# Last attention of a four-layer block: TensorE turns one unit in eight instead of one in four, VectorE and DMA turn all four units of every second half

## The reference

```python
xn = layer_norm(x, g1, b1)                    # x: the context, (4, 512, 256)
ln_lat = layer_norm(latents, g2, b2)          # latents: the tokens, (4, 512, 256)
q = ln_lat @ Wq                               # 16 heads of 64
kv = jnp.concatenate([xn, ln_lat], axis=1) @ Wkv      # 1024 keys
weight = jnp.einsum('bhld,bhnd->bhln', q * scale, k * scale)
weight = jnp.where(full_mask[:, None, None, :], weight, neg)
weight = jax.nn.softmax(weight.astype(jnp.float32), axis=-1)
out = jnp.einsum('bhln,bhnd->bhld', weight, v)
return out @ Wout
```

## Time and profile before

| | |
|---|---|
| runs | 2943.0, 2953.18, 2944.42 us; median 2944.42 |
| profiled execution | 2945.35 us, span 2943.6 |
| granted TensorE clock, mean | 0.92 of full |
| TensorE busy | 2481.0 us, 84% of the span |
| VectorE busy | 1828.4 us, 62% |
| ScalarE busy | 1170.7 us, 40% |
| GpSimd busy | 755.3 us, 26% |
| DMA | 257.06 MB, mean 87 GB/s |
| transfers of the last attention (L791) | 1024 of 96 KB: 784 by SyncE, 240 by ScalarE |

### The profile page before, as it was taken

How to read it: one execution, slowest core, us unless ns; L and a number is a source line. 1 busy time by engine, 2 the same in 40 slices (tenths; PEclk the granted TensorE clock), 3 DMA queues, 4 the chain that set the end, 5 groups by cost and what they waited for, 6 DMA issues and landing times. The chain is left out here.

```text
span 2943.6 us, 35609 instructions
## 1 busy us (share of the span) xinstructions
PE 2481.0 (84%) x12608; PEld 1335.9 (45%) x12608; DVE 1828.4 (62%) x4072; ACT 1170.7 (40%) x2095; POOL 755.3 (26%) x462
## 2 busy tenths in 40 slices
PE   6888972865888699889899979989988989997996
PEld 2333331323555344545554635554454545463554
DVE  5667745246867474477767357748437875835774
ACT  1433430212323153265544146635325653514662
POOL 1002352520000042043323023414203432402441
PEclk8999985875878799999999999999999999999998
DMA  7411006974200200244320124430023442012442
GB/s 226 136 37 21 11 15 206 316 249 150 87 8 3 106 1 1 87 108 119 97 79 8 73 61 118 116 111 11 8 88 100 116 108 79 1 52 71 110 125 73
DMA packets 112959, 257.06 MB, mean 87 GB/s; under 512 B 36198, under 2 KB 56294, under 8 KB 106762
## 3 DMA queue, kind: packets, MB, share of 16 engines
q1 hardware_dynamic: 93978, 220.26, 24.8%
q10 hardware_dynamic: 12656, 25.97, 3.6%
q0 software_dynamic: 6144, 8.48, 1.0%
HBM read 119.81 MB, written 29.69 MB: 51 GB/s over the span
## 5 line engine op out<-in xcount | busy, mean ns | idle before, releaser
L858 POOL TENSOR_SCALAR pbuf<-pbuf,recip 128x1024 f32<-128x1024 f32 x128 | 364.5, 2848 | 946.0 <-DVE recip L762 946.0
L807 ACT ACTIVATE pbuf<-ps,least 128x1024 f32<-128x1024 f32 x256 | 284.3, 1113 | 295.3 <-DVE least L755 219.5
L755 DVE CUSTOM_DVE_ANT_0 ps<-ps,mask 128x1024 f32<-128x1024 f32 x256 | 307.9, 1244 | 140.2 <-PE ps L687 139.2
L584 POOL TENSOR_SCALAR pbuf<-pbuf,recip 128x512 f32<-128x512 f32 x128 | 200.2, 1576 | 459.7 <-DVE recip L505 459.7
L687 PE MATMUL ps<-kH,qT 64*128 64x512 f32 x1024 | 267.4, 642 | 49.8 <-ACT pbuf L807 47.0
L712 PE MATMUL ps<-work,vh 128*64 128x256 f32 x2048 | 251.9, 390 | 0.0
L555 ACT ACTIVATE pbuf<-ps,least 128x512 f32<-128x512 f32 x256 | 172.7, 686 | 155.6 <-DVE least L495 155.6
L769 DVE STREAM_TRANSPOSE pbuf<-pbuf 128x2048 f32<-128x2048 f32 (+1 forms) x128 | 226.3, 1768 | 0.0
L1554 ACT ACTIVATE early<-ps 128x1536 f32<-128x1536 f32 x86 | 123.9, 1441 | 200.9 <-PE ps L1369 191.7
L1632 DVE TENSOR_REDUCE mh<-ps 128x3 f32<-128x1536 f32 x86 | 150.0, 1744 | 63.8 <-PE ps L1358 61.2
L712 PEld LDWEIGHTS ps<-work,vh 128*64 128x64 f32 x2048 | 138.3, 138 | 95.2 <-issue 36.6
(11 more groups left out here) (371 smaller groups left out, 4054.7 us busy)
## 6 DMA issues: line engine op xcount, KB each, us to landing
work<-pbuf SPq DMA_DIRECT2D x784, 96.0 KB, 2.5
work<-pbuf ACTq DMA_DIRECT2D x240, 96.0 KB, 2.9
early<-in_L_wgu SPq DMA_DIRECT2D x22, 768.0 KB
expert_rows<-zero_rows SPq DMA_DIRECT2D x16, 1024.0 KB, 11.5
yg<-expert_rows SPq DMA_DIRECT2D x16, 1024.0 KB, 6.0
early<-in_L_wd SPq DMA_DIRECT2D x22, 384.0 KB
arena<-in_L_wo SPq DMA_DIRECT2D x8, 1024.0 KB, 8.8
arena<-in_L_wff SPq DMA_DIRECT2D x4, 2048.0 KB, 9.3
```

The costliest lines, as they stand in the source:

```text
L584: nc.gpsimd.tensor_scalar(x, x, recip[:, n % 8:n % 8 + 1], None, mult).then_inc(probs_ready[1], 1)
L755: nc.vector.tensor_tensor_reduce(out=x, in0=x, in1=mask, scale=1.0, scalar=FMAX, op0=add, op1=ALU.min, accum_out=least[:, n % 8:n % 8 + 1])\
L807: nc.scalar.activation(to, x, ACT.Exp, bias=least[:, n % 8:n % 8 + 1], scale=-1.0, accum_out=sums[:, n % 8:n % 8 + 1]).then_inc(taken, 1)
L858: nc.gpsimd.tensor_scalar(unit(n), unit(n), recip[:, n % 8:n % 8 + 1], None, mult).then_inc(pool_divided, 1)
```

## The change

In an even half all stays. In an odd half the fourth unit (unit 8g+7) is no longer turned by TensorE and copied by ScalarE: the exponential writes it beside its three neighbours, VectorE turns it with the third unit in one instruction of 128x2048, and the transfers of that half carry four units (rows of 4096 B in place of 3072). Its place among the entries in PSUM goes, so that scores of step 1 follow those of step 0 directly. The last half of an attention is odd, so the turn at its end goes too. The number of transfers stays.

```diff
     def entry(n):
-        return n + max(0, n // 4 - 1)
+        return n + n // 8
 
     def entry_turned(h):
-        return min(4 * (h + 2), groups * per) + h
+        return min(4 * (h + 2), groups * per) + h // 2
 
     def unit(n):
-        return lasts[n // 4 % 2] if n % 4 == 3 else probs[n // 4 % 2][:, :, n % 4, :]
+        return last if n % 8 == 3 else probs[n // 4 % 2][:, :, n % 4, :]
 ...
         def values(h, part, of):
             g, half = divmod(h, 2)
             if part == 0:
                 pe.wait_ge(moved[h % 2], arrivals * (h // 2 + 1))
-                pe.wait_ge(taken, entry_turned(h) + 1)
+                if half == 0:
+                    pe.wait_ge(taken, entry_turned(h) + 1)
 ...
-            if p >= 2 and p % 2 == 0:
+            if p % 4 == 2:
                 turn_last(p // 2 - 1)
 ...
-        turn_last(N // 2 - 1)
-
 ...
         def turn(p):
             v.wait_ge(pool_divided, p + 1)
-            if p % 2 == 0:
+            first = 2 * p % 4
+            if p % 4 == 1:
+                x = unit(2 * p)
+            else:
                 v.wait_ge(act_divided, p + 1)
-            x = probs[p // 2 % 2][:, :, 0:2, :].rearrange("p j u r -> p j (u r)") if p % 2 == 0 else unit(2 * p)
+                x = probs[p // 2 % 2][:, :, first:first + 2, :].rearrange("p j u r -> p j (u r)")
             nc.vector.transpose(x, x).then_inc(turned, 1)
 ...
+        units = 3 + h % 2
         for a, j in pairs:
-            eng.dma_start(pts[h % 2][32 * j:32 * (j + 1), a, 0:3, :, :].rearrange("p u c q -> p (u c q)"),
+            eng.dma_start(pts[h % 2][32 * j:32 * (j + 1), a, 0:units, :, :].rearrange("p u c q -> p (u c q)"),
 ...
-            if p >= 2 and p % 2 == 0:
+            if p % 4 == 2:
                 keep_turned(p // 2 - 1)
 ...
-        keep_turned(N // 2 - 1)
 ...
-            pe.wait_ge(att3[6], HP * 2 * NT + HP * NT // 2 - 1)
+            pe.wait_ge(att3[6], HP * 2 * NT + HP * NT // 4)
```

More of the change, by code:

```diff
@@ L586, in attention_pairs, with attention_moved @@
     return tensor, vector, scalar, av_kept, jobs_kept, plan, divider
-def attention_moved(nc, sem, name, ps, ident, groups, q_of, k_of, v_of, mask, probs, lasts, pts, sums, recip, least, out,
+def attention_moved(nc, sem, name, ps, ident, groups, q_of, k_of, v_of, mask, probs, last, pts, sums, recip, least, out,
                     jobs):
@@ L686, in score @@
                     g, qt, s = where(n)
-                    last = nc.tensor.matmul(scores(n)[:, kb * BANK:(kb + 1) * BANK], q_of(g, s, qt), k_of(g, s, kb),
+                    product = nc.tensor.matmul(scores(n)[:, kb * BANK:(kb + 1) * BANK], q_of(g, s, qt), k_of(g, s, kb),
                                             start=True, stop=True)
                     if kb == 1:
-                        last.then_inc(scores_ready, 1)
+                        product.then_inc(scores_ready, 1)
         def turn_last(h):
@@ L695, in turn_last @@
             pe.wait_ge(act_divided, 2 * h + 2)
-            x = unit(4 * h + 3)
             for c in range(2 * NT):
-                last = nc.tensor.transpose(place(e)[:, c * P:(c + 1) * P], x[:, c * P:(c + 1) * P], ident)
-            last.then_inc(turned_tile, 1)
+                turn = nc.tensor.transpose(place(e)[:, c * P:(c + 1) * P], last[:, c * P:(c + 1) * P], ident)
+            turn.then_inc(turned_tile, 1)
         def values(h, part, of):
@@ L711, in values @@
                 for s in range(2):
-                    last = nc.tensor.matmul(ps[64 * s:64 * (s + 1), 6, half * 256:(half + 1) * 256], v_of(g, s, c),
+                    product = nc.tensor.matmul(ps[64 * s:64 * (s + 1), 6, half * 256:(half + 1) * 256], v_of(g, s, c),
                                             pts[half][:, :, s::2, c, :].rearrange("p a t q -> p t a q"),
@@ L715, in values @@
             if part == of - 1:
-                last.then_inc(av_ready, 1)
+                product.then_inc(av_ready, 1)
         score(0)
@@ L803, in exponent @@
             to, x = unit(n), scores(n).rearrange("p (j r) -> p j r", j=strips)
-            if n % 4 == 3:
+            if n % 8 == 3:
                 to = to.rearrange("p (c j k) -> p j c k", c=2 * NT, j=strips)
@@ L3042, in layers2to3 @@
                          lambda g, s, c: vh[g % 2][:, c, s * DH2:(s + 1) * DH2], mask3[:, :],
-                         [pbuf[:, 4 * i:4 * i + 3, :].rearrange("p x (y r) -> p (x y) r", r=256)
+                         [pbuf[:, 4 * i:4 * i + 3 + i, :].rearrange("p x (y r) -> p (x y) r", r=256)
                           .rearrange("p (j u) r -> p j u r", j=4) for i in range(2)],
-                         [pbuf[:, 4 * i + 3, :] for i in range(2)],
+                         pbuf[:, 3, :],
                          [work[:, i * 4096:(i + 1) * 4096].rearrange("p (x c q) -> p x c q", c=8, q=32)
```

4 lines of the change are left out of this document (2 added, 2 removed).

## The result

The changed kernel takes 3031.76 us (median of 4 runs, 3027.31 to 3035.56), the kernel before 2948.8 in the runs beside it (4, 2943.0 to 2954.33): a ratio of **1.0292 [1.0269, 1.0316]**, 2.9% slower. Forecast were 2978 us (1.1% slower) and a range up to 3006. The direction and the place were right, the size was two and a half times too small. The profiled execution took 3035.24 (span 3033.5), 89.9 more than that of before.

What follows compares the result with a forecast made beforehand. The prediction saw two bounds side by side: a loop through the odd half's turn and transfer landing, and TensorE's work. Terms 29.6 + 5.4 + 3.2 less 4.5 gave +33.7 us, 2978 us against the median; range 2966 to 3006.

Steps and rivals of the forecast that it cites:

- What bounds the kernel: Per group: loop of exponentials to odd half's turn, 17.7 us, then to transfers' landing, 9.2; TensorE's work about equal.
- The gain of TensorE's part: Eight products fewer per odd half, about 0.96 us each on the clock, falling outside the loop, so TensorE only waits longer.
- The turn, 1.08 a link: VectorE's double turn in odd halves adds 1.08 us to each link, the stretch from one odd half to the next.
- by the same 1.08, not more: ScalarE's own four transfers wait for the longer turn, so what stands behind them moves by 1.08 us only.
- The transfers: Odd halves' transfers, 96 KB to 128 KB: landing later by 0.4 us, between 0.1 and 0.9, in 20 links.
- a landing over 10.5 us: Sign of error: landing that far behind the odd half's turn would mean engines slower with large rows than assumed.
- The clock: Rival, chance 0.17: longer gaps lower TensorE's clock, some 1.45 us per fall in the loop; 2992 to 3014 us.
- The closes: Ends of the four attentions, where TensorE's last turn goes: 3 x 0.96 + 1.6 = 4.5 us gained.
- The sum: Over 28 links: 29.6 + 5.4 + 3.2 less 4.5 for the closes, together +33.7 us.
- That the landing doesn't bind: Rival, chance 0.11: ScalarE's and VectorE's own way to the exponential decides in all links; 2940 us, no change.
- That TensorE is the bound: Rival, chance 0.05: transfers only seem to end the waits; 31 us gained, 2914 us.
- The range: 2966 to 3006 us, leaving out the last two rivals (0.16) and the far end of the clock.

Runs made afterwards that it cites:

- TensorE's part alone: Changed kernel with VectorE's single turn and three-unit transfers restored in odd halves, fourth unit neither turned nor moved: 2957.29 us, 1.0004 against the kernel before.
- an earlier turn: Kernel before, with VectorE's turn of odd steps moved ahead of the next step's two minima: 2932.36 us, ratio 0.9933.
- the three-unit kernel: Changed kernel, but odd halves' transfers carry three units (96 KB), fourth unit turned but not moved; double turn stays: 2994.63 us, 1.0114 against the kernel before.
- the turn alone: Kernel before plus VectorE's double turn in step 3; TensorE's turns and 96 KB transfers stay: 2982.51 us, ratio 1.0092.
- the turn at its old length: Changed kernel, but VectorE turns only the third unit in odd halves; transfers stay at 128 KB: 3020.11 us, 1.0212 against the kernel before.
- the filler: Changed kernel plus two idle score products on TensorE in step 1, ahead of the value projection, from the second group on: 3031.34 us, 1.0245 against the kernel before.

## Why the prediction fell short

**What bounds the kernel** was right: the loop, with TensorE's own work close behind it. Taking TensorE's part alone gave 1.0004, an earlier turn 0.9933 and no more.

**The gain of TensorE's part** was rightly kept out of the loop. Whether losing it also costs something through the clock stays open: the three-unit kernel came out 11 us above the turn alone, inside the intervals of the two.

**The turn, 1.08 a link**: right, 27.1 us measured for 27.0. That ScalarE's own four issues shift what stands behind them "by the same 1.08, not more" was off by a little: behind an odd half's turn they took 2.76 in the mean before and 3.00 after, and single ones reach 3.97, as in the period shown above.

**The transfers** are the step that failed first: "I take 0.4, between the ends", 0.1 and 0.9. The runs showed 1.39, and 1.50 with the turn at its old length, so even the upper bound was too low. It was built on 254 GB/s, read in 3.00 us in which both queues issued. Over 6.90 us at a share of 0.95 the engines moved 237. The shortest landings are now 10.8; with the prediction's own 1.15 and 0.6 off, 2.10 MB in 9.05 us are 232 GB/s. The step also took the transfers as bound by their issue for the last two thirds, at 280 GB/s, a rate between two rows which none had shown for a move within SBUF; in the runs the issues themselves stretched, from 7.31 to 8.00 us. And it counted them in 20 links, 25 in its upper bound; all 25 ended on them. Together 25 x 1.39 = 35 us in place of 8. The text had named "a landing over 10.5 us" as what would show this.

**The clock** was the first rival, with a chance of 0.17 and 1.45 a fall. It came true on top of the forecast and isn't an alternative to it: 1.08 a link, 27 us, of which TensorE's slow rows account for 1.05 a link and the filler gave back 0.71. The argument against it, that the gap "would stay under the 2.76" of the earlier trace rows, took the one slow row as a threshold. Slow projections stand behind gaps of 2.22, with the filler even behind 1.66, and the gap grew by the landing, which was mis-sized. The Trainium skill, "TensorE: Matmul & The Clock Gate", section "HAM oscillation — how this bites in real kernels", has a loop in which a wait for transfers lowers the clock in each pass; the trace agrees in part, with 17 slow projections of 32.

**The closes**: forecast 4.5 gained, and there is nothing of it to be seen. From the last exponential of the last attention to the end it took 50.6 us, for 50.0 before. The output products waited again, now for ScalarE's copy of the result:

```profile
2985.07 1.95 PE L712 MATMUL ps<-work,vh 128*64 128x256 f32 x16
2987.59 6.28 PE L3071 MATMUL ps<-arena,wide 128*128 128x256 f32 x28 [0.57 <-ACT wide L829]
```

**The sum.** Turn 27 (forecast 27 of its 33.7), bytes 35 (8), clock 27 (0), the rest about 1 (-1.3): 90 of 89.9. The lengths of the four attentions, 241.5, 242.3, 241.9 and 240.1 against the ones above, add up to 90.9: by the starts of the odd halves' exponentials 10.2 in the first links of the four, 75.8 in the 21 behind them, 5.3 in the last links of the first three, where 3.2 were forecast.

**The other rivals.** That the landing doesn't bind: no, it ended the wait in all 25 links. That TensorE is the bound: no, by the kernel with TensorE's part alone. **The range** took the forecast and the clock as one or the other; it should have held the two together, 48 and 36 us, 3028, and even that is 4 below the measured time.

## What to carry over

When an engine is 97% busy, look in the chain for a loop through a buffer's reuse; add up its parts, and price a change by what it does to that loop alone. Before bytes are added to transfers that stand in such a loop, ask whether they are bound by their issue or by their engines, and take the rate from a stretch as long as the transfers will last. The wait that grew in front of TensorE cost twice here, in itself and in the clock of what follows; work taken from that engine was no gain there (1.0004), and rivals of this kind add up rather than exclude each other.

## What the hardware showed that I had not expected

- **A knee in transfer size.** Sixteen transfers from two queues land at the least 9.0 us after the turn with 64 KB each, 9.15 with 96 KB and 10.7 with 128 KB. At 64 and 96 KB the twelfth issue starts at the least 6.9 us after the first, 0.63 a step, so the issue sets the landing. At 128 KB it is never under 7.5, and the DMA engines' share over 6.90 us is 0.95 (237 GB/s), where the same length in before, 2741.00 to 2747.90, shows 0.87 (214 GB/s): there the engines set it. The Trainium skill, "DMA: Bandwidth & Descriptors", section "Issuing engines are not separate DMA queues", says that transfers of all issuing engines share the same sixteen. No run here tests that by itself; that ScalarE's four land 4.0 us after their issue with 128 KB, for 2.8 with 96, while SyncE's move beside them, fits it.
- **A full share is not one rate**: 254 GB/s over 3.00 us with rows of 3 KB, 237 over 6.90 us with rows of 4 KB. Which of the two differences does it, length or row, was not told apart.
- **Single issues stall.** One of SyncE's took 1.75 us where the others take 0.6, four of ScalarE's 3.97 where 2.9 is usual. What lets them wait isn't shown.
- **The length of the gap ahead doesn't tell the clock.** Behind the same 2.2 us of idle time one projection ran in 2.05 and another in 3.35, and with the filler one ran in 3.68 behind 1.66.
